# A softmax attention layer inside an eight-step kernel: the order of TensorE's and ScalarE's jobs within one software-pipelined slot

## What is computed

```python
q, k, v = h @ Wq, h @ Wk, h @ Wv          # h: layer-normed, modulated x
for each head and half r:                 # 16 heads x 2 halves
    p[r] = softmax(causal(q[r] @ k[r].T * scale))
o = (p[0] - lam * p[1]) @ v               # lam from lq1, lk1, lq2, lk2
o = rmsnorm(o) * (1 - LAMBDA_INIT)
x = x + ga * (o @ Wo)
```

## Time and profile before

| what | value |
|---|---|
| median of 3 runs | 2160.86 us (2156.38 to 2165.47) |
| the profiled execution | 2160.2 us, of which 2158.4 us are the span of the trace |
| mean granted TensorE clock over the span | 0.934 of full speed |
| busy share of the span | PE 86%, PEld 59%, DVE 64%, ACT 35%, POOL 41% |
| the third attention | about 670 to 1300 us of the span |

### The profile page before, as it was taken

One profiled execution on the slowest core, in us unless ns is written; L12 is line 12 of the kernel. 1 busy time (PEld: TensorE's weight loads), 2 busy tenths in 40 slices (PEclk: granted clock), 3 DMA queues, 4 the chain that ended last, 5 costly groups with the idle time before them and its releaser, 6 DMA issues.

```text
span 2158.4 us, 40010 instructions
## 1 busy us (share of the span) xinstructions
PE 1859.6 (86%) x13400; PEld 1273.0 (59%) x13400; DVE 1373.9 (64%) x3587; ACT 747.4 (35%) x1511; POOL 895.4 (41%) x965
## 2 busy tenths in 40 slices
PE   8999999689995888888888885899876788998887
PEld 5555555689983454544444434667665566886443
DVE  4767777365543555555555544888864776887776
ACT  2444444112222545545455450111122222443332
POOL 0354545565552435444344332322334223663333
PEclk7999999799997999999999997999999888999887
DMA  6100000100006553444544500000001100000111
GB/s 234 40 9 5 7 6 7 31 11 8 9 8 121 126 98 66 98 85 78 92 77 82 104 8 11 8 10 7 10 28 31 28 15 18 13 15 13 36 32 44
DMA packets 68177, 93.34 MB, mean 43 GB/s; under 512 B 9852, under 2 KB 62316, under 8 KB 64748
## 3 DMA queue, kind: packets, MB, share of 16 engines
q1 hardware_dynamic: 68076, 92.01, 18.9%
HBM read 61.70 MB, written 29.49 MB: 42 GB/s over the span
## 4 chain that ended last, share of the span: by engine, by line
PE 66%; DVE 18%; issue 7%; POOL 3%; ACT 3%; DMA 1%; DVEq 1%; SPq 0%; POOLq 0%; ACTq 0%
PE PS L1020 16%; PE PS L668 3%; PE PS L725 3%; PE PS L1965 3%; PE PS L1841 3%; PE PS L1175 2%; PE PS L741 2%; PE PS L507 2%; DVE xn L497 2%; PE PS L2004 2%; PE PS L1896 2%; PE PS L1893 2%; PE PS L722 2%; DVE negmax L2180 2%; PE PS L1938 2%
## 5 line engine op out<-in xcount | busy, mean ns | idle before, releaser
L2180 DVE TENSOR_REDUCE negmax<-PS 128x2 f32<-128x512 f32 (+1 forms) x384 | 247.2, 685 | 272.1 <-PE PS L1896 153.7
L538 POOL TENSOR_TENSOR X<-X,y_sb 128x512 f32 (+1 forms) x128 | 165.2, 1290 | 185.6 <-DVE y_sb L533 180.6
L533 DVE TENSOR_TENSOR y_sb<-PS,ga_sb 128x512 f32<-128x512 f32 x96 | 66.4, 691 | 195.3 <-PE PS L769 50.1
L2100 ACT ACTIVATE pw<-PS 128x512 f32<-128x512 f32 x256 | 139.1, 599 | 120.9 <-PE PS L1941 120.5
L1020 PE MATMUL PS<-we_hi,h_parts 128*128 128x512 f32 x512 | 179.9, 412 | 0.0
L497 DVE TENSOR_SCALAR xn<-X,mv,rs 128x256 f32 (+1 forms) x256 | 155.3, 648 | 22.5 <-POOL rs L490 21.2
L517 ACT ACTIVATE hT<-PS,modT 128x256 f32<-128x256 f32 x256 | 129.9, 558 | 106.0 <-PE PS L507 104.2
L1020 PE MATMUL PS<-l_h_parts,lut_hi 128*128 128x256 f32 (+1 forms) x768 | 145.4, 291 | 6.7 <-POOL l_h_parts L1143 6.7
L488 POOL TENSOR_TENSOR rs<-mv,eps 128x2 f32<-128x2 f32 x128 | 26.7, 208 | 294.5 <-DVE mv L481 294.3
L1509 DVE SCALAR_TENSOR_TENSOR l_acc<-PS,rt_g,l_acc 128x256 f32<-128x256 f32 x256 | 106.1, 475 | 30.8 <-PE PS L1020 25.8
L1020 PEld LDWEIGHTS PS<-l_h_parts,lut_hi 128*128 128x128 f32 (+1 forms) x768 | 117.8, 184 | 9.6 <-issue 5.4
(11 more groups left out here) (270 smaller groups left out, 4392.4 us busy)
## 6 DMA issues: line engine op xcount, KB each, us to landing
ga_sb<-ga_dram SPq DMA_DIRECT2D x128, 128.0 KB, 2.9
qk_dram<-qk_parts SPq DMA_DIRECT2D x64, 192.0 KB, 2.8
KS<-qk_dram SPq DMA_DIRECT2D x32, 384.0 KB, 6.0
QS<-qk_dram SPq DMA_DIRECT2D x32, 384.0 KB, 9.4
qk_dram<-qk_parts SPq DMA_DIRECT2D x64, 128.0 KB, 2.8
wmod<-in_wmod SPq DMA_DIRECT2D x4, 1536.0 KB, 14.9
qk_dram<-qk_parts SPq DMA_DIRECT2D x64, 64.0 KB, 2.5
y_out<-X SPq DMA_DIRECT2D x16, 256.0 KB, 2.2
```

What stands on the lines that cost most here:

```text
L538: pool.tensor_tensor(xb(b), xb(b), y_sb[b.par][:, :, :], ALU.add).then_inc(s.x.sem, 1)
L2100: act.activation(to.rearrange("p a n -> p (a n)"), bank(4 + (2 * n + pr) % 3), ACT.Exp).then_inc(s.prob.sem, 1)
L2180: dve.tensor_reduce(to, src, AX.X, ALU.max, negate=True).then_inc(s.max.sem, 1)
```

## The change

PE's order and ACT's order within `slot` of the third attention are changed; DVE's, POOL's and SP's are not. `by_token` on PE takes the group number and issues one group at a time. Nothing is added to or removed from the work.

```diff
-            def by_token(b):
-                pe.wait_ge(*s.oT(b))
-                for n in range(4):
-                    if n == 0:
-                        pe.wait_ge(*s.prob(b))
-                    if n == 3:
-                        pe.wait_ge(*s.u(b, 1))
-                    qt, gh = n // 2, n % 2
-                    for g in range(4):
-                        last_ = pe.transpose(...)
-                    last_.then_inc(s.otok_ps.sem, 1)
+            def by_token(b, n):
+                if n == 0:
+                    pe.wait_ge(*s.oT(b))
+                    pe.wait_ge(*s.prob(b))
+                if n == 3:
+                    pe.wait_ge(*s.u(b, 1))
+                qt, gh = n // 2, n % 2
+                for g in range(4):
+                    last_ = pe.transpose(...)
+                last_.then_inc(s.otok_ps.sem, 1)
...
# TensorE's slot
                 if i.ok:
                     max_pair(i, 0, 0)
+                if d.ok:
+                    exp_pair(d, 1, 2)
                 if c.ok:
                     project_k(c)
                 if d.ok:
                     exp_pair(d, 2, 0)
-                    exp_pair(d, 2, 1)
                 if i.ok:
                     max_pair(i, 0, 1)
                 if d.ok:
                     values(d, 1)
+                    exp_pair(d, 2, 1)
+                if i.ok:
+                    max_pair(i, 0, 2)
+                if d.ok:
                     exp_pair(d, 2, 2)
-                if i.ok:
-                    max_pair(i, 0, 2)
                 if c.ok:
                     project_q(c)
...
                 if i.ok:
                     max_pair(i, 2, 0)
-                    max_T_first(i)
                 if d.ok:
                     values(d, 3)
                 if i.ok:
+                    max_T_first(i)
                     max_pair(i, 2, 1)
+                    max_pair(i, 2, 2)
                 if c.ok:
                     project_v(c)
-                if i.ok:
-                    max_pair(i, 2, 2)
                 if d.ok:
-                    by_token(d)
-                if i.ok:
-                    exp_pair(i, 0, 0)
+                    for n in range(3):
+                        by_token(d, n)
+                if i.ok:
                     max_pair(i, 3, 0)
+                if d.ok:
+                    by_token(d, 3)
                 if e.ok:
                     out(e)
                 if i.ok:
-                    for n in (1, 2):
-                        exp_pair(i, 0, n)
-                        max_pair(i, 3, n)
+                    exp_pair(i, 0, 0)
+                    max_pair(i, 3, 1)
+                    exp_pair(i, 0, 1)
+                    max_pair(i, 3, 2)
+                    exp_pair(i, 0, 2)
                 next_tokens(i)
                 if i.ok:
                     exp_pair(i, 1, 0)
                     values(i, 0)
                     max_T_second(i)
                     exp_pair(i, 1, 1)
-                    exp_pair(i, 1, 2)
...
# ScalarE's slot
+                if d.ok:
+                    exps(d, 1, 2)
                 if c.ok:
                     evict_qk(c, 1, s.k_ps, s.k, 1.0)
                 if d.ok:
                     exps(d, 2, 0)
+                    copy_oT(d, 1)
                     exps(d, 2, 1)
-                    copy_oT(d, 1)
                     exps(d, 2, 2)
...
-                if i.ok:
-                    copy_maxT(i, 0)
                 if d.ok:
                     copy_oT(d, 3)
+                if i.ok:
+                    copy_maxT(i, 0)
...
                     copy_maxT(i, 1)
                     exps(i, 1, 1)
-                    exps(i, 1, 2)
```

More of the change, by code:

```diff
@@ L1968, in values @@
                 last_.then_inc(s.pv.sem, 1)
-            def by_token(b):
-                pe.wait_ge(*s.oT(b))
-                for n in range(4):
-                    if n == 0:
-                        pe.wait_ge(*s.prob(b))
-                    if n == 3:
-                        pe.wait_ge(*s.u(b, 1))
-                    qt, gh = n // 2, n % 2
-                    for g in range(4):
-                        last_ = pe.transpose(bank(4 + n % 3)[:, g * P:(g + 1) * P], l1_oT[:, 4 * gh + g, qt * P:(qt + 1) * P], ident[:, :])
-                    last_.then_inc(s.otok_ps.sem, 1)
+            def by_token(b, n):
[6 more added lines that the diff above has]
+                for g in range(4):
+                    last_ = pe.transpose(bank(4 + n % 3)[:, g * P:(g + 1) * P], l1_oT[:, 4 * gh + g, qt * P:(qt + 1) * P], ident[:, :])
+                last_.then_inc(s.otok_ps.sem, 1)
             def normed_T(b):
@@ L2027, in slot @@
                     values(d, 1)
-                    exp_pair(d, 2, 2)
+                    exp_pair(d, 2, 1)
                 if i.ok:
                     max_pair(i, 0, 2)
+                if d.ok:
+                    exp_pair(d, 2, 2)
                 if c.ok:
@@ L2053, in slot @@
                 if i.ok:
+                    max_T_first(i)
                     max_pair(i, 2, 1)
+                    max_pair(i, 2, 2)
                 if c.ok:
                     project_v(c)
+                if d.ok:
+                    for n in range(3):
+                        by_token(d, n)
                 if i.ok:
-                    max_pair(i, 2, 2)
+                    max_pair(i, 3, 0)
                 if d.ok:
-                    by_token(d)
-                if i.ok:
-                    exp_pair(i, 0, 0)
-                    max_pair(i, 3, 0)
+                    by_token(d, 3)
                 if e.ok:
@@ L2135, in slot @@
                     act.activation(l1_ogT[:, :, :].rearrange("p k t -> p (k t)"), bank(0), ACT.Copy).then_inc(s.ogT.sem, 1)
+                if d.ok:
+                    copy_oT(d, 3)
                 if i.ok:
                     copy_maxT(i, 0)
-                if d.ok:
-                    copy_oT(d, 3)
                 if c.ok:
```

## The result

The changed kernel takes 2096.11 us in the median of 4 runs (2095.8 to 2101.8), the kernel before 2163.16 us in the same session (2156.38 to 2166.34, 4 runs): a ratio of 0.9702, 95% interval [0.9676, 0.9728]. That is 67 us less, where 60 were forecast (2100.5 us from 2160.9). The profiled execution is the slowest of the four, 2101.8 us, with a span of 2100.0 us against 2158.4.

A forecast was written before the change was run, and what follows sets the result against it. PE's work plus its pauses (4.88 of 38.53 us a slot) bound the stage. -3.2 us a slot gives -45 over 14 slots, clock -13, last slots -2: -60 on 2160.2, forecast 2100.5 us, range 2090 to 2127.

The forecast's parts named there:

- Steps 1, 2 and 3: PE slot: moving exponent pairs (1, 2), (2, 1) and values (3) removes pauses: -0.5, -1.17, -1.05 us.
- Step 3: Values (3) ahead of the first maxima transposes: -1.05 us a slot; the later copy of the maxima on ACT free.
- Step 4: Maxima pair (2, 2) right behind (2, 1): two such pairs in a row cost a pause, +0.68 us a slot.
- Step 5: Fourth token group behind maxima pair (3, 0), 0.87 us of work against a 0.59 pause: -0.59 us a slot.
- Step 6: Output projection (1.93 us) ahead of exponent pair (0, 0), hiding its wait on DVE's fourth token group: -1.25 us a slot.
- Step 7: DVE late next behind the token groups: +0.4 us before maxima pair (3, 2), +0.3 before pair (1, 0).
- Steps 8, 9 and 10: 0.24 before pair (2, 0) stays; second-half maxima rows free by 0.25 us; stacked Q read free by over 2 us.
- Slot 0: First slot of the third attention, which has neither d nor e: forecast to change by nothing.
- The last slots: Last two slots: same pauses with fewer fillers, slot 15 paying more for the maxima rows: -2 us.
- The clock, -13: Clock falls follow only the close pauses 0.59 and 1.25; both go, so no falls: 8 x 1.6 = 13 us less.
- the clock still falls: Rival: clock falls in about as many slots, behind new pauses or on its own; 2113 us, chance 0.22.
- The slower rival: Exponent pair (2, 0) waits for second-half maxima DMAs; loses once latency is over 6.6 us; 2180 us, chance 0.03.

The follow-up runs named there:

- the four parts: Kernel before with one part each: (1, 2) moved, (2, 1) moved, values (3) first, tokens split and output first; ratios 0.9928, 0.9893, 0.9902, 0.9869.
- (2, 0) early: Changed kernel with exponent pair (2, 0) ahead of project_k on PE and its exponents ahead of the copy of k on ACT; 2128.4 us, 0.9844.
- the case of 2.8 against 3.4 us: (2, 0) early: PE idle 2.8 us a slot, clock falls in slots 3, 7, 8; tokens split and output first: 3.4 to 3.6, none in slots 2 to 13.
- the filler: Kernel before with redundant matmuls (first half of values (1), computed once more) between exponent pairs (2, 0) and (2, 1); 2177.1 us, 1.0078.

## Why the prediction was right, and where it wasn't

- *The bound* (PE's work plus PE's pauses, no other engine near full): held. 3.64 us of pauses went together, and 3.73 us of the slot; alone, the four parts took 0.7 to 1.3 us off it.
- *Steps 1, 2 and 3*: the three waits are gone. Alone these parts shorten the slot by 0.8, 0.9 and 0.7 us where 0.5, 1.17 and 1.05 were forecast, 2.4 in sum against 2.7.
- *Step 3, "free" on ACT*: not quite. It costs 0.20 before project_v wherever (2, 2) doesn't lie between.
- *Step 4, +0.68*: exact, and the price of something that the prediction didn't see, DVE's early start on the token groups.
- *Step 5, -0.59 by splitting the token groups*: the wait went but for another reason; without the split it is gone too. The prediction had "DVE is free for group 0 as soon as it comes" in the very sentence, and didn't draw that this alone removes the wait.
- *Step 6, -1.25*: confirmed by undoing it, 0.7 to 1.0 net of the wait at (3, 2) that comes with it.
- *Step 7*: 0.4 before (3, 2) measured 0.32. The 0.3 before pair (1, 0) isn't seen: the pair starts 1.61 behind (0, 2) (904.46 to 906.07), as worked out, but the transposes between them end only 0.09 before that, since the last f32 transposes run on for 0.66. This and the small differences make 34.80 of 35.3.
- *Steps 8, 9 and 10*: the 0.24 stayed; the maxima rows have 0.25 us of margin; nothing waits for the stack in mid-stage. Slot 0, forecast at nothing, cost 2.2. The last slots, forecast at -2, gave 0.7 beside the full slot. Of the missing 1.3 the waits for the maxima rows are 1.2 (3.2 us where 2.0 were), a cost that the prediction named and set too low.
- *The clock, -13*: 12.8 in the slots. The size was right, by luck in part. The reading of the rows was mostly right: all eight falls follow the two close pauses (seven make a long slot, not eight; the eighth is in slot 1). The inference was wrong. Those pauses needn't go for the falls to stop, as each other single part ended most of them; nor is their going enough, since slot 1 of the kernel with the tokens split and the output first has a fall of 7 us, and with (2, 0) early others came. So the rival "the clock still falls" was argued against with half a reason. The Trainium skill (Perfetto Trace Analysis, Matmul Optimizations) says that the matmul engine scales its power with utilization. The ends agree: falls in 8 slots of 13 with 4.8 to 5.0 us of pauses in 38.5, in none with 1.24 in 34.8. Which slots are long doesn't, other than the prediction says: slots 6 and 10 have the same pauses, and one is long. Nor does the case of 2.8 against 3.4 us above.
- *The slower rival*: its mechanism and price are real, shown by the kernel with (2, 0) early; its condition, a latency over 6.6 us, is far from the measured 3.1. (Its 2180 us are the 20 us of loss alone; with the 13 of the clock off, as its own words have it, they are 2167.)

## What to carry to other kernels

Write each pause of the bounding engine with its releaser beside the jobs that could fill it, and lay out the new order in microseconds until the first job that is late next. Here that gave 60 of 67 us. When two edits lie near one pause, ask of each whether the other already removes it. Where the clock falls behind pauses, as here, the first one filled may pay for most falls, so single edits overstate themselves and don't add. And read the ends of a pipeline by themselves: the job that hides a wait in mid-stage is missing in the last slots.

## What the runs showed that was not expected

With the filler, PE stood still at the loop's turns. In each of the three turns between the loop's four passes PE's timeline has rows like these, before the first maxima pair and in the middle of it:

```profile
899.30 1.03 PE L1882 MATMUL PS<-later,ident_b 128*128 128x512 bf16 x2 [3.03 <-issue]
902.08 0.61 PE L1885 MATMUL PS<-KS,QS 48*128 48x128 bf16 x8 [1.75 <-issue]
```

The slots there take 44 to 46 us, and the clock is at 0.50 from 898 to 906 us. The DMA queue that brings instructions moved 89 packets in this kernel; it is 61 in the kernel before and in the changed one:

```profile
q8 instruction: 89, 1.46, 0.3%
```

The added instructions are 528 in 40,538. That the loop's body had just outgrown what is kept of it, and was fetched anew at each turn, fits the 28 packets more and the place of the pauses, but it is a guess: no kernel was run to show it. A redundant instruction in a loop isn't a clean probe of a pause.
